# Transposing the attention's q, k and next tokens by DMA instead of on TensorE, with six unread matmuls where a batch's heads begin

## What is computed

```python
# attention: 16 heads of 16, rotary q and k, blocks of 64 tokens, all earlier blocks and the own one
q = _rope(q)
k = _rope(k)
scores = jnp.einsum('bhqd,bhkd->bhqk', q, k) * SCALE
scores = jnp.where(tok_mask[None, None], scores, -jnp.inf)
attn = jax.nn.softmax(scores, axis=-1)
ctx = jnp.einsum('bhqk,bhkd->bhqd', attn, v)
return ctx @ w_o.T
# feed-forward: of every 4 neighbouring hidden values the 2 largest in magnitude are kept
h = jax.nn.silu(jnp.einsum('bsh,hi->bsi', x, w_gate)) * jnp.einsum('bsh,hi->bsi', x, w_up)
h_sparse = _sparsify_2to4(h)
return jnp.einsum('bsi,ih->bsh', h_sparse, w_down)
```

## Time and profile before

| | value |
|---|---|
| median of 3 runs | 1810.37 us |
| the profiled execution | 1815.68 us, its span 1813.9 us |
| PE busy | 1541.0 us (85%) |
| DVE busy | 1153.2 us (64%) |
| ACT busy | 821.9 us (45%) |
| POOL busy | 220.9 us (12%) |
| mean granted PE clock | 0.922 of full speed |
| the phase's last load, w_fd, issued by SP | at 688.7 us |
| first x tile of batch 0 turned | at 702 us |
| first exponential of batches 0 to 3 | at 795.3, 1060.1, 1324.6 and 1593.2 us |

### The profile page before, as it was taken

How to read it: one execution, slowest core, us unless ns; L and a number is a source line. 1 busy time by engine, 2 the same in 40 slices (tenths; PEclk the granted TensorE clock), 3 DMA queues, 4 the chain that set the end, 5 groups by cost and what they waited for, 6 DMA issues and landing times.

```text
span 1813.9 us, 27446 instructions
## 1 busy us (share of the span) xinstructions
PE 1541.0 (85%) x10490; PEld 877.8 (48%) x10491; DVE 1153.2 (64%) x2401; ACT 821.9 (45%) x1352; POOL 220.9 (12%) x236
## 2 busy tenths in 40 slices
PE   4999999869989973689888989788989788889796
PEld 2666666545568871233354534255433344433345
DVE  5666677545420145678568678678778578778475
ACT  5445555313112213347854157753177663167530
POOL 2343444302410001000000000100000100000000
PEclk8999999879998986669999989999989999989999
DMA  2001010024124402000000000000000000000000
GB/s 107 13 24 36 23 31 27 12 80 117 39 64 141 132 1 96 1 1 1 1 1 1 0 1 1 25 1 1 1 1 1 25 1 0 1 1 2 24 1 24
DMA packets 27153, 48.04 MB, mean 26 GB/s; under 512 B 7312, under 2 KB 16016, under 8 KB 26256
## 3 DMA queue, kind: packets, MB, share of 16 engines
q1 hardware_dynamic: 26464, 44.74, 7.6%
q0 software_dynamic: 576, 1.77, 0.3%
HBM read 37.59 MB, written 9.06 MB: 26 GB/s over the span
## 4 chain that ended last, share of the span: by engine, by line
issue 60%; POOL 2%; DVE 0%; POOLq 0%; DVEq 0%
POOL rs_sb L1340 1%; POOL ve_sb L1337 0%; POOL qks_sb L1355 0%; POOL v_sb L1354 0%; POOL qks_sb L1345 0%; DVE bn_sb L1545 0%; DVE x_sb_sb L1560 0%; POOLq L1159 0%; POOLq L66 0%; POOL qks_sb L1356 0%; DVE mv_sb L1551 0%; DVEq L1159 0%; POOL v_sb L1353 0%; DVE ident_h_sb L1742 0%; DVEq L66 0%
## 5 line engine op out<-in xcount | busy, mean ns | idle before, releaser
L1612 DVE TENSOR_REDUCE mx_sb<-s_ps 128x1 f32<-128x512 f32 (+1 forms) x512 | 313.1, 652 | 116.1 <-PE s_ps L1906 67.8
L1418 ACT ACTIVATE room_sb<-s_ps 128x1024 f32<-128x1024 f32 (+1 forms) x320 | 283.2, 948 | 24.0 <-PE s_ps L1930 22.9
L1903 PE MATMUL s_ps<-room_sb 48*128 48x512 f16 (+3 forms) x640 | 177.2, 345 | 37.8 <-DVE mx_sb L1607 18.7
L1930 PE MATMUL s_ps<-room_sb 51*128 51x128 f16 (+4 forms) x1152 | 145.9, 283 | 22.7 <-ACT room_sb L1418 15.1
L1950 PE MATMUL cm_ps<-room_sb,v_sb 128*32 128x512 f32 (+3 forms) x1536 | 162.8, 513 | 0.8 <-ACT room_sb L1424 0.8
L1903 PEld LDWEIGHTS s_ps<-room_sb 48*128 48x128 f16 x640 | 52.8, 95 | 208.8 <-DVE mx_sb L1612 124.9
L2072 PE MATMUL cm_ps<-w_fd_sb,room_sb 128*128 128x256 f32 x512 | 132.3, 407 | 14.7 <-DVE room_sb L1694 14.7
L1337 POOL TENSOR_TENSOR ve_sb<-mv_sb,eps_sb 128x4 f32<-128x4 f32 x24 | 5.0, 210 | 1086.2 <-DVE mv_sb L1551 1086.2
L396 DVE SCALAR_TENSOR_TENSOR x_sb_sb<-xp_sb,conv_w_sb,x_sb_sb 128x512 f32<-128x512 f32 x96 | 106.6, 1113 | 22.6 <-ACT x_sb_sb L319 20.5
L2072 PEld LDWEIGHTS cm_ps<-w_fd_sb,room_sb 128*128 128x128 f32 x512 | 97.8, 199 | 38.9 <-issue 14.1
L2059 PE MATMUL s_ps<-xbT_sb,w_fg_sb 128*128 128x512 f16 x384 | 100.9, 393 | 10.3 <-DVE ctok_sb L1660 8.7
(11 more groups left out here) (256 smaller groups left out, 3034.6 us busy)
## 6 DMA issues: line engine op xcount, KB each, us to landing
we_gu_sb<-we_gu SPq DMA_DIRECT2D x32, 352.0 KB
we_dn_sb<-we_dn SPq DMA_DIRECT2D x32, 176.0 KB
x_in_sb<-x SPq DMA_DIRECT2D x9, 512.0 KB, 3.5
rows<-x_sb_sb SPq DMA_DIRECT2D x8, 512.0 KB, 3.0
x_sb_sb<-rows SPq DMA_DIRECT2D x2, 2048.0 KB, 11.5
out<-x_sb_sb SPq DMA_DIRECT2D x8, 512.0 KB, 2.6
xp_sb<-w_in SPq DMA_DIRECT2D x1, 1024.0 KB, 7.9
x_sb_sb<-w_up SPq DMA_DIRECT2D x1, 1024.0 KB, 8.6
```

The source lines that it names most:

```text
L1418: act.activation(weights[(g * NU + u) % SLOTS_P][:, 2 * pair:2 * pair + 2, 0:width(u) * P], W[s % 2][:, :, 0:width(u) * P], ACT.Exp, scale ...
L1612: dve.tensor_reduce(mx[:, pair, k % 2, slot:slot + 1], X[:, k % 2, 0:count * P], AX.X, ALU.max, negate=True).then_inc(mx_ok, 1)
L1903: last = pe.matmul(X[:, k % 2, at * P:(at + plain) * P], query[head:head + NORM, i * P:(i + 1) * P], key[head:head + NORM, j * P:(j + plai ...
L1930: last = pe.matmul(W[s % 2][:, head, (at + low - i) * P:(at + high - i) * P], key[first:first + rows, j * P:(j + 1) * P], query[first:firs ...
```

## The change

- q and k (without maxima) and the x tiles are transposed by DMA, SBUF to SBUF, issued by SP (`x_turned`, `turned_rows`). Gone are `x_transposed`, `xt_copied`, `rows_transposed` for these, `qk_copied`, and their waits. q with its maxima is still turned by PE (`q_max_transposed`).
- `qks` is laid out so that one transfer takes a pair's 128 x 1024 values: 2 (q or k) x 8 pairs x 8 tiles x 2 heads x 64. `w_qk` is ordered to fit, on the host.
- `heads` begins with `scores(b, 0, 0)`, then six matmuls of 512 columns into a bank that nobody reads (`kept_busy`), then `q_max_transposed(b, 0, 1)`. The 6 maxima ahead of step 0 are gone; steps 0 to 7 do 3 each, the later ones 2 (`AHEAD` is 8).
- DVE waits for all five late constants (`w_o` and `w_fd` too) before the prologue's rotations. The output store of a batch stands behind the next batch's last transposing transfer.

```diff
-AHEAD = 6
+AHEAD = 8
@@
-        qks = sb("qks", [P, ST, NHG * 2 * HG, FW], F16)
+        qks_flat = sb("qks", [P, 2 * NHG * 2 * ST * 2 * FW], F16)
+        qks = qks_flat[:, :].rearrange("p (s g t h f) -> p s g t h f", s=2, g=NHG * 2, t=ST, h=2)
@@ max_jobs
-            return (g + 1, AHEAD + 2 * s) if AHEAD + 2 * s < 2 * NX else (g + 2, AHEAD + 2 * s - 2 * NX)
+            if g == 0 and s < AHEAD:
+                return ((1, 3 * s, 3 * s + 3),)
+            low = AHEAD + 2 * s
+            return ((g + 1, low, low + 2),) if low < 2 * NX else ((g + 2, low - 2 * NX, low - 2 * NX + 2),)
@@ sync
+            def x_turned(c, t):
+                k = c * ST + t
+                wait(sync, xs_low, k + 1)
+                wait(sync, qkv_mm, k - 1)
+                sync.dma_start_transpose(xt[:, t % 2, :, :, :].rearrange("p a f c -> p (a f) c"),
+                                         xs[:, t % 2, :, :].rearrange("p a c -> p (a c)")).then_inc(xt_in[t % 2], 16)
+
+            def turned_rows(b, g, pair):
+                n = b * NHG + g
+                before = n - (3 if pair == 0 and g == 3 else 2)
+                if g == 0:
+                    wait(sync, sc_mm, STEPS * n)
+                elif g == 3 or (g, pair) == (2, 1):
+                    wait(sync, sc_mm, STEPS * (before + 1))
+                wait(sync, qk_in[pair], 32 * n)
+                for tiles, s in ((kT, 1), (qT, 0)):
+                    sync.dma_start_transpose(of_pair(tiles, g, pair).rearrange("p (t c) -> p t c", t=ST),
+                                             rows_of(g, s, pair)).then_inc(qk_in[pair], 16)
@@
+            for b in range(NB):
+                for t in range(ST):
+                    x_turned(b, t)
+                wait(sync, ca_ok, (b + 1) * ST)
+                wait(sync, low_ok, (b + 1) * ST)
+                wait(sync, zeroed, b + 1)
...
+                for pair in range(2):
+                    turned_rows(b, 0, pair)
+                wait(sync, hs_ok, 4 * b)
+                turned_rows(b, 1, 0)
+                turned_rows(b, 1, 1)
+                turned_rows(b, 2, 0)
+                turned_rows(b, 2, 1)
+                turned_rows(b, 3, 0)
+                turned_rows(b, 3, 1)
+                if b > 0:
+                    stored(b - 1)
+            stored(NB - 1)
@@ scalar, x_high (vector, x_low, alike)
-                wait(act, tx, k - 1)
+                if k > 1:
+                    xt_landed(act, k - 2)
@@ tensor, qkv
-                wait(pe, xt_ok, k + 1)
+                xt_landed(pe, k)
@@ tensor, for_maximum
-                    wait(pe, kq_ok, q(4, 4 if g == 0 else 2 * pair + 2))
+                    wait(pe, qk_in[pair], q(32, 32))
@@ tensor
+            def kept_busy(bank, count):
+                for i in range(count):
+                    pe.matmul(bank, ident_h[:, :], w_qk[:, 0, 0, :], start=True, stop=True)
+
             def heads(b):
                 scores(b, 0, 0)
-                qk_transposed(b, 1, 0, 1)
-                wait(pe, qm_ok, group(b, 0)(2, 1))
-                qk_transposed(b, 1, 0, 0)
-                for_maxima(b, 1, 0, AHEAD)
+                kept_busy(S[1][:, 0, :], 6)
                 q_max_transposed(b, 0, 1)
```

More of the change, by code:

```diff
@@ L1342, in zero_columns @@
             def zero_columns(c):
-                wait(pool, tm_mm, 2 * NHG * c)
-                for g in range(NHG):
-                    last = pool.memset(qks[:, :, g * 2 * HG:g * 2 * HG + HG, NORM:FILTER], 0.0)
-                last.then_inc(zeroed, 1)
+                all_q_max_turned(pool, c)
+                pool.memset(all_rows[:, 0, :, NORM:FILTER], 0.0).then_inc(zeroed, 1)
             pool.memset(power[:], -0.5)
@@ L1491, in _ @@
             part_copies(0, ST - 1)
-            for pair in range(2):
-                for s in (1, 0):
-                    qk_copied(0, 0, pair, s)
             q_max_copied(0, 0, 0)
@@ L1516, in _ @@
                 for w in range(16):
-                    if ahead and w + 2 < ST:
-                        xt_copied(c, w + 2)
                     if w == HALF_AT:
@@ L1620, in max_parts @@
                 wait(dve, joined, q(2, pair + 1))
-                own = slice(g * 2 * HG + 2 * pair, g * 2 * HG + 2 * pair + 2)
-                parts = [qks[:, :, own, NORM + c] for c in range(2)]
+                parts = [qks[:, 0, 2 * g + pair, :, :, NORM + c] for c in range(2)]
                 least = mx[:, pair, :, 0:ST].rearrange("p h t -> p t h")
@@ L1725, in heads @@
                             normalised(b, g, 0)
-                        of, m = max_jobs(g, s)
-                        if of < NHG:
-                            maxima(b, of, m, m + 2)
+                        for of, low, high in max_jobs(g, s):
+                            if of < NHG:
+                                maxima(b, of, low, high)
                         if g == NHG - 1:
@@ L1957, in sums_transposed @@
                 wait(pe, ev_ok, group(b, g)(2, LEAD + half + 1))
+                wait(pe, cn_ok, group(b, g)(2, LEAD + half))
                 for t in range(GT):
@@ L2088, in _ @@
             pe.wait_ge(ready, 2)
-            for pair in range(2):
-                first_rows(0, pair)
             for_maxima(0, 0, 0, NX + 4)
@@ L2098, in among_hidden @@
                 def among_hidden(w, i):
-                    if ahead and w + 2 < ST and i == 1:
-                        x_transposed(c, w + 2)
                     if ahead and w in (10, 11):
@@ L2114, in _ @@
                 heads(b)
-                if ahead:
-                    x_transposed(c, 0)
                 if b == 0:
-                    pe.wait_ge(late, 16 * 2)
+                    pe.wait_ge(consts, 16 * 5)
                     pe.wait_ge(w_low, 4)
@@ L2141, in _ @@
                         qkv(c, w + 2)
-                    if ahead and w in (NF, NF + 1):
-                        first_rows(c, w - NF)
                 down(b, 2, nothing)
```

203 lines of the change are left out of this document (63 added, 140 removed).

## The result

The changed kernel took 1818.69 us at the median of 8 runs (1814.62 to 1821.14), against 1805.27 us (1802.75 to 1812.74) for the kernel before in the same comparison: a ratio of 1.0065, 95% interval 1.0047 to 1.0083. It is slower by about 12 us, where 1764 us was forecast. The two profiled executions are nearly level (1814.62 and 1815.68 us): the changed kernel's is the fastest of its eight runs, the other is above all of its, and the first layer, which the change doesn't touch, took 7 us less in the changed kernel's execution (the phase begins at 694.3 us, before at 701.5). So I compare stages, not totals.

What follows compares the result with a forecast made beforehand. PE was taken to set the pace in the heads with maxima, DVE close behind. Heads -30, feed-forward -12 and prologue -8 made -50 us from 1815.7, the median at 1760; 1764 us was predicted, range 1738 to 1822.

Steps and rivals of the forecast that it cites:

- They hold PE 8.06 us together, so 8/13 of it, 5.0 us, goes with them.: Heads with maxima: removing 8 of 13 groups of transposes from PE shortens 74.9 us to 69.9 a batch.
- Rival 1: Heads: DVE takes PE's place as the limit, so only entry and prologue pay; 1797 us, chance 0.14.
- The entry, -3.4 us: Start of the heads, until the 24th maximum: 19.7 us become 16.3 a batch, if PE has its full clock.
- The step more for the last stage, +0.9: Last heads, the stage without maxima: one step more there costs 0.9 us a batch.
- The unread matmuls: Entry of the heads: six matmuls where PE waits for DVE anyway, costing 0 to 2.6 us, taken as 0.
- Rival 4: Entry: unread matmuls don't hold the clock, which stays 0.74, and cost 2.6 us more; 1788 us, chance 0.62 together with the forecast.
- The feed-forward, -4 us a boundary: Between batches: removing transposes and their waits for ACT saves 4 us a batch, -12 in three batches.
- The prologue, -8 us: Prologue: with x by DMA rotations come 4.1 us apart, five periods save 12.7 us, some taken back: -8.
- also some 6: Prologue's end: two transfers of q and k replace the 6.0 us from last low part to first maximum; change 0.
- The transfers at 3.5 us: Transposing DMAs of q and k, 256 KB each: 3.5 us taken, between 2.6 and 10, all hidden.
- rivals 2 and 3: Transposing transfers land late: at 10 us each, 1890 us, chance 0.14; at 5.5 to 7.5, about no change, chance 0.10.
- rival 3: Gain and late transfers cancel, one transfer taking 5.5 to 7.5 us: 1780 to 1825 us, chance 0.10.

Runs made afterwards that it cites:

- e2_pre6: The changed kernel with the order of maxima of the kernel before (6 ahead of step 0, then 2 a step): 1807.26 us, ratio 0.9996.
- e3_discarded: The changed kernel with eight unread transposes put back on PE in steps 3, 5, 13 and 15 of the heads, without copies: 1827.0 us, ratio 1.0116.
- e14_fill_heads: e2_pre6 with the missing transposes put back, results unread, in the heads alone: 1797.45 us, ratio 0.9941 to the kernel before.
- e15_split_pre6: e2_pre6 with the weighted matmuls of a four-tile unit in two halves, the second in the odd step: 1790.06 us, ratio 0.9915.
- e6_split_before: The kernel before with the weighted matmuls of a four-tile unit issued in two halves, the second a step later: 1836.81 us, ratio 1.0147.
- e1_ahead6: The changed kernel with AHEAD = 6 instead of 8: 1809.94 us, ratio 1.0000 to the kernel before.
- e4_no_busy: The changed kernel without the six unread matmuls (`kept_busy`): 1822.29 us, ratio 1.0084 to the kernel before.
- e7: e2_pre6 with all missing transposes put back, results unread, in the heads and between the batches: 1801.4 us, ratio 0.9951.
- e13: e2_pre6 with the missing transposes put back, results unread, between the batches alone: 1804.79 us, ratio 0.9976.
- e9_x0_dma: The kernel before with x turned by DMA in the prologue alone: 1794.47 us, ratio 0.9942.
- e5_x_dma: The kernel before with x alone turned by DMA, in the prologue and between the batches: 1803.95 us, ratio 0.9970.

## Why the prediction was wrong

By its own steps:

- **"They hold PE 8.06 us together, so 8/13 of it, 5.0 us, goes with them."** This step failed: it measured 0. It took PE's busy share of 92% as a sign that PE sets the pace. e2_pre6 against before (30.42 and 30.43 us a group), e3_discarded against after (31.36 and 31.36) and e14_fill_heads show the transposes free at the full clock, and the timelines show why: they lay in a wait beside the loop. e15_split_pre6 against e6_split_before tests it: with the loop shortened they cost 2.4 us a group (the two runs also differ in ScalarE's copies and the transfers). The trace of before had it: a step of 2.1 us follows one of 1.2, and PE waits for DVE in the short one. Rival 1, DVE in the place of PE, had the right sign for this step, though neither engine alone is the bound.
- **The entry, -3.4 us.** It measured 0 (20.0, 20.0, 20.0, 19.2 us). The new order of maxima was priced only there; in the steady groups I had put it at nothing. It costs 0.94 us a group at the full clock, and e1_ahead6 gets 0.65% of the time back, some 12 us. This term alone makes the difference between no change and slower. The step more for the last stage, +0.9, measured +0.3.
- **The unread matmuls.** Rival 4, that they don't hold the clock, was right for the entry: 0.58 granted against 0.74. Instead of the 10 us that it added for their own time they cost nothing, and saved about 3 (e4_no_busy, whose interval overlaps the changed kernel's).
- **The feed-forward, -4 us a boundary.** It failed: the three lost 5.0 us. At an equal 13.7 us of half clock the stretch took 145.9 to 146.7 us without transposes (the changed kernel and e14_fill_heads) and 146.4 to 149.6 with them (before, e7 and e13), so 1 to 2 us may be there, not 4, and the clock took them back. DVE is busy 112 us of it either way, and from the first to the last of the eight rotations in it went 42.2 us in all three boundaries after, 42.2 to 43.3 before. That fits a pace set by DVE; no run shows it by itself.
- **The clock.** The sum put at nothing, without a reason, that the clock falls when the edit takes work from PE. At half clock the phase ran 173.7 us before and 224.3 after, and putting unread transposes back into the heads is worth 0.55% (0.9996 to 0.9941), 10 us.
- **The prologue, -8 us**, was right and a little small: -11.5. Rotations stand 3.7 to 4.6 us apart now, where 4.1 was said, and from the last low part to the first maximum it took 5.4 us, where "also some 6" was said. From the timeline of DVE after, against the earlier trace rows:

```profile
702.25 0.69 DVE L1601 TENSOR_TENSOR ro_sb<-qk_sb,cos_sb 128x512 f32<-128x512 f32 x1 [4.01 <-ACT v_sb L1439]
706.64 0.68 DVE L1601 TENSOR_TENSOR ro_sb<-qk_sb,cos_sb 128x512 f32<-128x512 f32 x1
...
733.84 0.42 DVE L1614 TENSOR_TENSOR qks_sb<-ro_sb,qks_sb 128x256 f16<-128x256 f32 x1
```

- **The transfers at 3.5 us** were right, so rivals 2 and 3 had no cause. The 1309 ns for one 128 x 128 block that the Trainium skill has in "VectorE: DVE Perf Modes" (The three transpose paths) would make, as an estimate, 10.5 us of the eight blocks in a transfer; the trace has 3.4. "Advanced Engine Details and Errata" (X-Bar Transpose), by which they are as fast as plain ones, is much nearer: of the plain ones, loads of 256 KB took 4.4 and 7.9 us here and stores of 512 KB 2.6.
- **The range.** 1818.69 us lies inside 1738 to 1822, and that is luck: its upper part stood for transfers that land late (rival 3, T between 5.5 and 7.5 us), and they landed in 3.4. The sum itself came to 1760; nothing in it gives the 4 us up to 1764.

The parts add up: prologue -10.5 us (0.58% by e9_x0_dma), order of maxima +12, lost clock +10, together +11.5; measured +11.8 (0.65% of 1809). By the intervals each carries 4 to 5 us of uncertainty, so that they meet within 0.3 us is chance; and they were not tried one by one on the same base.

Open stays what exactly decides the clock between two batches. e9_x0_dma took 152.9 and 146.4 us for the same work in two batches of one run; with x by DMA, e5_x_dma took 153.7 and 155.2 there and e14_fill_heads 146.7 twice. Also open is how ScalarE's copies double the price of the bad order (32.41 against 31.36 us); unread transposes without copies left it at 31.36.

## What to carry to other kernels

A high busy share doesn't show that an engine is the bound: before you credit the removal of an instruction, look whether the same engine stands waiting right behind it. Where it does, find the loop of waits through both engines and shorten what lies on it; the edit that removed the transposes became worth something in the heads only once the block on the loop was split (0.9996 to 0.9915, a third of it by the loop itself). Look at the clock as well: work that costs nothing where it stands may be what keeps it up. And price an order of work for every step that it touches, in the steady part first.
